# Expert results scattered by GpSimd to their tokens' rows and loaded as plain rows; gate product on VectorE

## The reference

```python
x = layernorm(x + causal_attention0(x))          # 16 heads of 64
x = layernorm(x + cross_attention0(x, ctx))      # 120 context rows, one head
x = layernorm(x + moe(x))                        # the block of this change
x = layernorm(x + gated_attention1(x))           # 16 heads of 16, clocks, gates, rotations, then an MLP
x = layernorm(x + cross_attention1(x, ctx))      # 4 heads
x = layernorm(x + rwkv_mix(x))
# moe: 8 experts, 2 for each token
gate = xf @ gate_w
weights, sel = top_k(gate, 2); weights = softmax(weights)
h = dense_1_w x + dense_1_b                      # 1024 per expert: gates at even places, values at odd
g, v = min(h[0::2], 9), clip(h[1::2], -9, 9)
h = g * sigmoid(1.702 * g) * (v + 1)
y = dense_2_w h + dense_2_b
out = sum over the two chosen experts of weight * y
```

## Time and profile before

| | |
|---|---|
| median of 3 runs | 1195.58 us (1195.24 to 1195.78) |
| the profiled execution | 1197.88 us, with a span of 1196.1 us |
| mean granted clock of TensorE | 0.97 |
| busy over the span | PE 1098.9 us (92%), PEld 792.6 (66%), DVE 718.9 (60%), ACT 551.1 (46%), POOL 474.6 (40%) |
| expert block | about 474.6 to 699.5 us of the span |
| last block | from 699.57 us |
| transfers of the change | 39 stores of 128 KB by ScalarE, 39 row gathers of x and 32 gathers of results by GpSimd |

### The profile page before, as it was taken

The page is one execution under the profiler, slowest core; times in us unless marked ns, Lnnn a source line. Parts: engine busy times, 40 slices in busy tenths (PEclk is TensorE's granted clock), DMA queues, the critical chain, the costliest instruction groups (busy, mean ns, idle before and its releaser), DMA issues. The chain is left out here.

```text
span 1196.1 us, 20449 instructions
## 1 busy us (share of the span) xinstructions
PE 1098.9 (92%) x6772; PEld 792.6 (66%) x6772; DVE 718.9 (60%) x2197; ACT 551.1 (46%) x1399; POOL 474.6 (40%) x551
## 2 busy tenths in 40 slices
PE   9899989998999897999999988699899999998997
PEld 4476557645754676999999965455555665575875
DVE  1482376247524846555655647749849787956367
ACT  1381255217421834333333328367476557643542
POOL 0160034006400885666666547515432442323023
PEclk9999999999999899999999989589999999999999
DMA  6000200020002014951111135000100100000001
GB/s 209 19 1 1 60 19 2 0 60 19 1 0 61 2 61 144 323 163 46 50 49 45 45 110 185 6 1 9 28 1 17 36 2 26 10 1 19 1 1 36
DMA packets 39997, 55.85 MB, mean 47 GB/s; under 512 B 6758, under 2 KB 32166, under 8 KB 39894
## 3 DMA queue, kind: packets, MB, share of 16 engines
q1 hardware_dynamic: 30598, 39.61, 10.1%
q0 software_dynamic: 3408, 9.31, 2.8%
q10 hardware_dynamic: 5888, 5.64, 1.5%
HBM read 43.76 MB, written 10.78 MB: 46 GB/s over the span
## 5 line engine op out<-in xcount | busy, mean ns | idle before, releaser
L1821 PE MATMUL bank<-words 128*128 128x256 f32 (+3 forms) x872 | 268.3, 459 | 17.7 <-ACT words L2428 3.3
L1821 PEld LDWEIGHTS bank<-words 128*128 128x128 f32 (+1 forms) x872 | 163.9, 194 | 96.0 <-issue 58.9
L464 PE MATMUL bank<-words 128*128 128x512 f32 x384 | 171.1, 594 | 0.2 <-issue 0.2
L409 POOL TENSOR_TENSOR words<-words 128x256 f32<-128x256 f32 (+1 forms) x128 | 102.5, 830 | 152.7 <-DVE words L1090 152.2
L1297 PEld LDWEIGHTS bank<-words 128*128 128x128 f32 x1248 | 145.8, 192 | 3.5 <-ACT words L1333 1.6
L1297 PE MATMUL bank<-words 128*128 128x128 f32 x1248 | 146.3, 276 | 0.9 <-ACT words L1333 0.9
L787 ACT ACTIVATE words<-words 128x128 f32<-128x128 f32 (+1 forms) x256 | 112.9, 443 | 33.5 <-DVE words L923 33.5
L464 PEld LDWEIGHTS bank<-words 128*128 128x128 f32 x384 | 71.0, 190 | 78.5 <-issue 78.2
L779 ACT ACTIVATE words<-bank 128x512 f32<-128x512 f32 x48 | 28.7, 597 | 177.8 <-PE bank L464 177.8
L1348 ACT ACTIVATE words<-words 128x1024 f32 x39 | 41.1, 1057 | 137.1 <-PE bank L1297 113.2
L913 DVE COPY words<-bank 128x512 f32<-128x512 f32 x48 | 33.2, 691 | 91.9 <-PE bank L464 91.6
(11 more groups left out here) (366 smaller groups left out, 2050.8 us busy)
## 6 DMA issues: line engine op xcount, KB each, us to landing
words<-in_w SPq DMA_DIRECT2D x8, 1024.0 KB, 9.9
y_slots<-words ACTq DMA_DIRECT2D x39, 128.0 KB, 1.7
words<-in_w SPq DMA_DIRECT2D x8, 512.0 KB, 10.1
words<-in_x SPq DMA_DIRECT2D x4, 512.0 KB, 4.2
x_rows<-words SPq DMA_DIRECT2D x16, 128.0 KB, 1.8
words<-in_wm SPq DMA_DIRECT2D x2, 1024.0 KB, 7.2
out_x<-words SPq DMA_DIRECT2D x16, 128.0 KB, 1.8
words<-in_xt SPq DMA_DIRECT2D x3, 512.0 KB, 3.9
```

Of the source, the lines that this page charges most:

```text
L409: last = pool.tensor_tensor(part, part, inv[:, j % SLOTS0, :, t:t + 1].to_broadcast([P, 2, P * (t + 1)]), ALU.mult)
L464: last = pe.matmul(bank[c % 2][:, :], w, r, start=k == 0, stop=k == KD - 1)
L1821: last = pe.matmul(out, w, r, start=i == 0, stop=i == len(pairs) - 1)
```

## The change

1. The expert results no longer go to `y2` in slot order. GpSimd scatters each slot tile's 128 rows, by an indirect DMA with the offsets `home`, to the row of their token in a region of `y2` for first or second choices; slots without a token go to their own slot's row in a region ahead (RETURNED). ScalarE issues no store. The scatter stands last in GpSimd's iteration and waits for `yread`.
2. `home` is computed at the end of routing by VectorE: `token` numbers now carry RETURNED and the choice, `source` gets a mask, and three further steps make `home`. The base subtraction and the five steps at the head of the expert block are gone, with `slot`.
3. The product of gate and sigmoid moves from GpSimd to VectorE, in front of `hidden`.
4. GpSimd no longer waits for the stores at the end of the expert block; SP waits for them at the head of the last block.
5. All 32 gathers of results in the last block are gone from GpSimd. SP loads plain rows: group 0 first, group 1 behind the context's stores, group 2 in the second period, group 3 between the context's key and value loads.

```diff
+RETURNED = -(-SLOTS // (B * S)) * B * S
-            for v, pattern, step in (..., (token, [[P, TILES]], 1), ...):
+            pool.iota(token[:, :, :], pattern=[[B * S, 2], [P, TILES]], base=RETURNED, channel_multiplier=1, ...)
...
-                dve.tensor_tensor(keep["base"][:, :], end[:, :], length[:, :], ALU.subtract)
...
-            dve.tensor_copy(keep["source"][:, :], bank[0][:, 0:SLOT_TILES]).then_inc(routed, 1)
+            dve.tensor_copy(keep["source"][:, :], bank[0][:, 0:SLOT_TILES])
+            dve.drain()
+            dve.tensor_scalar(keep["source"][:, :], keep["source"][:, :], B * S - 1, None, ALU.bitwise_and).then_inc(routed, 1)
+            dve.tensor_scalar(owner[:, :], number[:, :], float(P), index[:, 0:1], ALU.mult, ALU.add)
+            dve.drain()
+            dve.scalar_tensor_tensor(owner[:, :], bank[0][:, 0:SLOT_TILES], 0.0, owner[:, :], ALU.is_equal, ALU.mult)
+            dve.drain()
+            dve.tensor_tensor(keep["home"][:, :], bank[0][:, 0:SLOT_TILES], owner[:, :], ALU.add)
             last_shares(0)
             last_shares(1)
...
                     copy_values(j + 2)
-                pool.wait_ge(gated, j + 1)
-                pool.tensor_tensor(sig[:, :], gate[:, :], sig[:, :], ALU.mult).then_inc(mixed, 1)
-            pool.tensor_copy(keep["l_at"][:, :, :], keep["slot"][:, :, 0:NT])
+                pool.wait_ge(yread, j + 1)
+                pool.indirect_dma_start(dram["y2"][:, :], bass.IndirectOffsetOnAxis(ap=home[:, j:j + 1], axis=0),
+                                        y[:, j % 2, :], None).then_inc(ystored[j % 2], 16)
...
-            for s in range(2):
-                pool.wait_ge(ystored[s], 16 * ((SLOT_TILES + 1 - s) // 2))
...
-                act.wait_ge(yread, j + 1)
-                act.dma_start(dram["y2"].rearrange("(j p) n -> p j n", p=P)[:, j, :], y[:, j % 2, :]).then_inc(ystored[j % 2], 16)
...
-            for r in range(2):
-                dve.tensor_tensor(chosen[:, r, :, :], chosen[:, r, :, :], base..., ALU.mult)
-            dve.tensor_reduce(first[:, :, :], chosen[:, :, :, :], AX.X, ALU.add)
-            dve.scalar_tensor_tensor(rank[:, :, :], first[:, :, :], float(P), rank[:, :, :], ALU.mult, ALU.add)
-            dve.tensor_copy(keep["slot"][:, :, :], rank[:, :, :])
...
-                dve.drain()
-                dve.wait_ge(mixed, j + 1)
+                dve.wait_ge(gated, j + 1)
+                dve.tensor_tensor(sig[:, :], gate[:, :], sig[:, :], ALU.mult)
+                dve.drain()
                 dve.scalar_tensor_tensor(hidden[:, s, :], value[:, :], -8.0, sig[:, :], ALU.max, ALU.mult).then_inc(hready, 1)
...
+            def load_returned(g):
+                if g >= 2:
+                    sp.wait_ge(vmm, NT * (g - 1) + NT)
+                    sp.wait_ge(qkmm, NT * (g - 1) + NT)
+                for n in (r * NT + t for t in range(NT) for r in range(2)):
+                    first = RETURNED + n // NT * B * S + (NT * g + n % NT) * P
+                    sp.dma_start(returned(g, n), dram["y2"][first:first + P, :]).then_inc(backed[g % 2][n % NT], 16)
+            for s in range(2):
+                sp.wait_ge(keep["ystored"][s], 16 * ((SLOT_TILES + 1 - s) // 2))
+            load_returned(0)
             for g in range(G - 1):
                 sp.wait_ge(ckr, 2 * g + 2)
                 sp.dma_start(dram["kx"][g], keptk[:, g, :]).then_inc(cstored, 16)
                 sp.dma_start(dram["vx"][g], keptv[:, g, :]).then_inc(cstored, 16)
+            load_returned(1)
...
+                if p == 1:
+                    load_returned(2)
                 if z is not None:
-                    load_context(z + 1)
+                    load_context(z + 1, 3 if p == 2 else None)
...
-            def gather(g):
-                ...
-                    pool.indirect_dma_start(returned(g, n), None, dram["y2"][:, :], ...).then_inc(backed[n], 16)
-            gather(0)
...
-                if b == 0:
-                    gather(1)
...
-                if a is not None and a + 1 < G:
-                    pool.wait_ge(vmm, NT * a + NT)
-                    gather(a + 1)
...
-                dve.wait_ge(backed[n], 16 * g + 16)
+                dve.wait_ge(backed[g % 2][t], 32 * (g // 2) + 32)
```

More of the change, by code:

```diff
@@ L960, in rank @@
                 for r in range(2):
[L961 removed]
+                    dve.tensor_tensor(picked[:, r, own, :], keep["chosen"][:, r, own, :],
                                       bank[3 if b is None else SUMMED[b]][:, 0:number * NE].rearrange("p (t e) -> p t e", t=number), ALU.mult)
@@ L1197, in expert_layer @@
         bias = b1[:, :, :].rearrange("p e c -> p (e c)")
-        ident, chosen, rank, base, owneri, source = (keep[n] for n in ("ident", "chosen", "rank", "base", "owner", "source"))
-        first = sb([P, 2, TILES])
+        ident, owneri, source, home = (keep[n] for n in ("ident", "owner", "source", "home"))
         ARRIVING = 20
@@ L1590, in load_context @@
                 sp.dma_start(kxt[:, :, :], dram["kx"].rearrange("g p (k n) -> g p k n", k=KD)[g]).then_inc(cloaded, 16)
+                if following is not None:
+                    load_returned(following)
                 if g:
@@ L1627, in _ @@
         def _(pool):
-            def gather(g):
-                if g > 0:
-                    pool.tensor_copy(at[:, :, :], keep["slot"][:, :, bass.ts(g, NT)])
-                    pool.drain()
-                for n in (r * NT + t for t in range(NT) for r in range(2)):
-                    pool.indirect_dma_start(returned(g, n), None, dram["y2"][:, :],
-                                            bass.IndirectOffsetOnAxis(ap=at[:, n // NT, n % NT:n % NT + 1], axis=0)).then_inc(backed[n], 16)
             def add_rows(g, r, out):
@@ L3342, in decoder @@
         keep["weight"] = memory.take([P, TILES, 2])
-        keep["slot"] = memory.take([P, 2, TILES], I32)
         keep["ident"] = memory.take([P, P])
@@ L3346, in decoder @@
         keep["at"] = memory.take([P, TILES, 2])
-        keep["chosen"], keep["rank"], keep["base"] = memory.take([P, 2, TILES, NE]), memory.take([P, 2, TILES]), memory.take([P, NE])
-        keep["owner"], keep["source"] = (memory.take([P, SLOT_TILES], I32) for _ in range(2))
+        keep["chosen"], keep["rank"] = memory.take([P, 2, NT, NE]), memory.take([P, 2, TILES])
+        keep["owner"], keep["source"], keep["home"] = (memory.take([P, SLOT_TILES], I32) for _ in range(3))
         first = memory.mark
@@ L3351, in decoder @@
         keep["behind"] = memory.mark
-        keep["rows_mark"] = memory.mark + 2 * TILES
+        keep["rows_mark"] = memory.mark
+        keep["ystored"] = [memory.sem(f"ystored{s}") for s in range(2)]
         keep["e_rows"] = cut(memory.words, keep["rows_mark"], (AHEAD_ROWS, D))
@@ L3359, in decoder @@
         keep["l_minus_half"], keep["l_eps"] = memory.take([P, 4, NT]), memory.take([P, NT])
-        keep["l_at"], keep["l_rows_in"] = memory.take([P, 2, NT], I32), memory.take([P, 2 * 1024])
+        keep["l_rows_in"] = memory.take([P, 2 * 1024])
         assert memory.mark <= Memory.WORDS
```

37 lines of the change are left out of this document (17 added, 20 removed).

## The result

The changed kernel takes 1204.57 us (median of 5 runs, 1202.82 to 1207.67), the kernel before 1195.78 beside it. The ratio, taken over all runs and not from the two medians, is 1.0057, 95% interval 1.0037 to 1.0076: about 0.6% slower, clear of the noise, and outside the predicted range of 1193.0 to 1201.8. The profiled execution took 1202.82 us; the one before took 1197.88.

The account below looks back on a forecast made before the run. TensorE was taken to bound the expert stage (busy 50.00 of 50 us), but not the last layers' first period. Terms 0.45 + 0.9 + 1.2 - 0.5 - 0.2 = +1.85 on the median 1195.58 gave 1197.4 us; range 1193.0 to 1201.8.

Parts of the forecast that it names:

- Block boundary: Expert block to last block: GpSimd issues scatter and fills, store landing becomes SP's wait; -0.5 us, between -0.7 and 0.
- my remaining 1.7: Block boundary: the gap expected in the profile after the change, 1.7 us, against 2.2 before.
- Routing: End of routing: four VectorE instructions ahead of the last shares start TensorE later; +0.9 us, between 0.7 and 1.2.
- The scatter on GpSimd's queue: Expert tiles: gathers behind the scatter land late only while weights stream in, steady tiles covered; +1.2 us.
- Last tile: Last expert tile: gate product stands behind the value clips on VectorE, TensorE waits; +0.45 us, between 0.3 and 0.5.
- gate product: Steady expert tiles: product takes 0.69 us on VectorE, covered by 2.4 us of slack; price 0.
- Last layers: Start of the last layers: SP's plain loads arrive before ScalarE is free for the rows; price 0.
- first period: First period of the last layers: GpSimd's adds move about 1.1 us earlier beside VectorE; -0.2 us, between -1.5 and +1.2.
- A: Expert weight stream: gather queues behind the scatter, +4 to +8 us instead of 1.2, about 1200 to 1204; chance 0.18.
- C: First period: VectorE's freed steps keep TensorE's clock up from 740 to 780; -4.4 us, 1193.0; chance 0.18.
- Its second half: Behind the block boundary: a shorter gap keeps the clock up, gaining half of five us; part of C's chance.
- D: First period: GpSimd's earlier adds collide with VectorE's chain; +1.2 us in place of -0.2, 1198.8; chance 0.08.

Follow-up runs that it names:

- Experiments 1: Changed kernel with the two fills and GpSimd's drain moved from behind the expert loop to ahead of it; 1204.76 us, ratio 1.0042 to the kernel before.
- experiment 10: Changed kernel with fills and drain ahead of the last scatter but one, plus a drain in tile 20 ahead of its scatter; profiled execution 1198.25 us, 2.2 above its median.
- 3: Changed kernel with GpSimd waiting for all scatters to land before the fills and drain; single execution, 1206.64 us.
- 4: Changed kernel with one more GpSimd drain, in tile 19 of 39; single execution, 1203.84 us.
- 8: Kernel before with its drain at the end of the expert block moved behind the wait for the stores; single execution, 1198.66 us.
- experiment 12: The changed kernel again, unaltered, on another chip beside further variants; its measured time is not given.
- experiment 7: Kernel before with only the product of gate and sigmoid moved to VectorE; 1196.99 us, ratio 0.9992 to the kernel before.
- experiment 2: Changed kernel with one more GpSimd drain in every tile, ahead of the wait for the result; 1209.36 us, ratio 1.0069 to the kernel before.
- experiments 5: Changed kernel with fills and drain ahead of the expert loop, and from tile 12 a drain behind each wait for the result; 1200.56 us, ratio 1.0019.
- 6: As experiments 5, plus gate product back on GpSimd, target rows computed in the expert block, each scatter issued one tile later; 1228.79 us, ratio 1.0248.

## Why the prediction was wrong, point by point

**Block boundary (-0.5): the step that failed.** The prediction said that GpSimd "issues the scatter (0.98 to 1.46), two small fills, and passes the boundary (0.39...)". The drain behind the fills was in the code and got no price. It measured 6.46 us and the step +5.96. Experiments 1 and 10 show that this drain is the gap, 3 and 4 that its length follows the count of indirect DMAs, whether or not their transfers are over, 8 that before it was hidden beside the last tile and the wait for the stores. The sign of the rest was right: without the drain the gap is 0.4, so that the landing moved to SP's wait is worth -1.8, more than the -0.5 that I gave it. The scatter's issue, which my remaining 1.7 contained, is then not waited for either: in 10 it runs from 699.18 to 700.14, TensorE from 699.31. I had looked at what the drain's neighbours cost by rows; a queue's instruction that has no row was taken for one without time. The earlier trace rows had a boundary of 2.2 us that I filled with one cause, the store's landing; that was right for the kernel before, but I did not ask what GpSimd did meanwhile.

**Routing (+0.9): right mechanism, +1.20 from cast to filler.** The four steps took 0.96. The rest, 0.25, is in the last shares behind them: one of their steps, at 472.25, takes 0.37 where its like takes 0.16; why is open. The handover is what it was, 0.38.

**The scatter on GpSimd's queue (+1.2): right that steady tiles cost nothing, too dear at the start.** One gather was late, by 0.33 us. A gather's issue takes 978 ns where it took 1457 in the earlier trace rows, and the scatter 992. From filler to last result the changed kernel took +0.72 in one profile and +0.25 in another (experiment 12). With the last tile's +0.39 in that, little is left for gathers. (The cover of a steady gather was 609.4 - 602.9 = 6.5, not 6.4; it changes nothing.)

**Last tile (+0.45) and gate product (0 in the steady stage): right.** 0.39 by rows in the changed kernel (clips end at 692.82, last step at 693.49; the earlier trace rows have 0.28 there), the same in experiment 7, and VectorE's load 35.20 where 36 was worked out.

**Last layers and first period (0, -0.2): -0.63 in all in the one profile, -0.05 in experiment 12's.** Within the spread of the stage.

**The rivals.** A (gathers queue behind scatters, 1200 to 1204) came nearest in time for the wrong reason: the only wait for rows is 0.33. C (clock kept up) did not come: 0.73 from 740 to 780 against 0.67. Its second half, a clock kept up behind a shorter boundary, came in experiment 10, and the last block is no shorter for it:

```profile
700.00:702.00 2.00, 2.00 (x11) 1.80 (x10) 0.00 (x0) 1.13 (x2) 0.14 (x1) 1.00 0.19 66
```

The granted clock is 1.00 where the earlier trace rows have 0.50, and the 48 products of L1821 take 10.28 in place of 13.26; yet the last block takes 497.17 in place of 496.57. Experiment 7 has the same 10.28 and 496.37. For D (GpSimd beside VectorE's chain) the rows of the first period, for the earlier trace rows:

```profile
745.51 1.35 POOL L1709 TENSOR_TENSOR words<-words 128x512 f32<-128x512 f32 x1 [5.19 <-ACT words L2520]
746.58 0.83 DVE L3040 TENSOR_TENSOR words<-words 128x512 f32<-128x512 f32 x1 [0.86 <-ACT words L2551]
746.84 5.12 POOL L1689 TENSOR_SCALAR words<-words 128x256 f32<-128x256 f32 x4
747.33 1.48 DVE L3048 TENSOR_TENSOR words<-words 128x512 f32<-128x512 f32 x2
...
758.29 1.28 POOL L1695 TENSOR_TENSOR words<-words 128x512 f32<-128x512 f32 x1
758.64 1.49 DVE L3016 TENSOR_TENSOR words<-words 128x512 f32<-128x512 f32 x1
```

Two of VectorE's two-operand steps are held by a GpSimd add, where one alone takes 0.69: 0.83 (to 747.41; the add ends at 746.86) and 1.49 (to 760.13; the add ends at 759.58). Both end 0.55 behind the end of the add, and so do the 1.35, 1.57 and 1.15 of the earlier trace rows. The Trainium skill's rule of the shared port (SBUF — State Buffer, "SBUF: two separate sides") agrees with these five. Beside scalings it does not come out as I priced it: the second step of L3048 takes 0.88, no step is held for most of a scaling, and the scalings get longer instead, 5.12 for four against 3.64 before. The step that took 1.57 runs free (0.69 at 769.93), so the last block is no longer for all this. No rival named a drain. My range was built of the costs that I had found, with none for a kind of instruction that I had not priced.

## What to carry to other kernels

When a change adds indirect DMAs to GpSimd's queue, find every drain on that queue and what must be done before it: price the next one by the DMAs since the last (here 0.08 us each), and put it where the engine idles with its transfers landed, in two or three parts if the idle times are short. A boundary's length in the profile of before has several covers; list what each engine does in it, instructions without rows included, before saying what goes when one cover goes. And a scatter that waits for a result must not stand, in the queue, between two products on which that result depends.

## What the runs showed of the hardware

- A drain on GpSimd takes time in proportion to the indirect DMAs issued since the last one, though all have landed: 3.27 us for 39, 6.46 for 78 (also 6.46 after a wait for the landing), 3.54 for 42, 3.01 for 36, 6.30 for 76, 2.85 for 34, 2.11 for 25, 0.72 for 8, 0.21 for 2; 0.05 for none. All lie within 0.05 of 0.05 + 0.082 for each DMA. What the engine does in that time was not looked into.
- A drain shortly behind a gather lasts more than its count: mostly 3.5 to 4.5 us with the weight stream running and mostly 0.8 to 1.9 after it, for two DMAs (experiment 2). It waits for their transfers: all 40 drains of that expert block end 0.41 to 0.77 us behind the last packet of an indirect DMA, and those of experiments 5 and 6 whose transfers were over last 0.21.
- The row of an indirect DMA on GpSimd is its issue (0.95 us for the last scatter), while the landing comes 2.4 us after the issue. The Trainium skill says the same of the end of such a row (Perfetto Trace Analysis, "DMA Instruction — SWDGE (GPSIMD)"): it is the end of making descriptors and not of the transfer.
- The gather's issue fell from 1457 to 978 ns with the changed work beside it. Before, 35 of the 36 gathers ran beside a two-operand step of VectorE over 128x512 and took 1453 to 1460; the one that did not took 978. In experiment 7, without GpSimd's multiply, 35 ran beside two such steps and took 1283 to 1353, the other 977. In the changed kernel none does, and all take 974 to 982.
- A VectorE step over two operands that a GpSimd add holds ends 0.55 us behind the end of the add, in five cases of the first period (0.83 to 1.57 us in place of 0.69).
